# Attention and experts on one core: row-maximum scores for two banks at a time, by the halves of TensorE's rows

## The chip, the cores and the metric

The kernel runs as one program on one core of a Trainium2 chip. The metric is the time of one execution on the device, in microseconds (us); the median of three runs before the change is 1871.49 us.

## The reference

```python
def attn(x, Wq, bq, Wk, bk, Wv, bv, Wo, bo, rel_k, rel_v):      # 16 heads of 8, M = 128
    r = jnp.arange(S)
    idx = jnp.clip(r[None, :] - r[:, None], -M, M) + M
    content = jnp.einsum('bhqd,bhkd->bhqk', q, k)
    relative = jnp.einsum('bhqd,qkd->bhqk', q, rel_k[idx])
    w = jax.nn.softmax((content + relative) / jnp.sqrt(jnp.float32(hd)), axis=-1)
    out = jnp.einsum('bhqk,bhkd->bhqd', w, v) + jnp.einsum('bhqk,qkd->bhqd', w, rel_v[idx])
    ...
x = x + layernorm(attn(layernorm(x), ...))                      # x: 16 x 512 x 128
x = x + layernorm(experts(layernorm(x), ...))                   # top 1 of 16 experts, and a shared one
```

Every query has 16 heads and 512 keys. A key further than 128 positions from its query takes one of two constant relative rows, a nearer one takes the row of its distance.

## The kernel before

There are two phases, each in a block of its own (`nc.Block()`), in which every engine follows its own list and engines wait for each other on semaphores only. The first phase is attention, the second the routed experts.

Attention works on pairs of batches, in eight turns. A turn i has 128 slots. In slot s TensorE computes the scores of one tile of 32 queries against 128 keys, for 16 heads (`scores`, L723 and, where the query tile t = s//32 and the key tile j = s//8%4 differ by at most 1, also L730), ScalarE takes their exponentials (L932), and at every odd slot TensorE multiplies two earlier slots' exponentials with the values (`values`, L749, and L756 for near tiles; its tile lags by one group of eight slots). The scores bank pair is `sc[0]`, `sc[1]`.

The softmax needs the maximum of each row beforehand. In the same slot, for the next turn's batches, `natural` computes the scores of 8 queries by 16 heads (128 rows) against all 512 keys into one bank of `mix`: L704 the content with the keys near the queries, L705 the relative part against the table `Wn`, and L707 and L709 the content with the keys to the left and to the right, which have a constant relative row added. Each has 128 rows of contraction, 128 columns of weights (`Qb`: queries masked by head, `Qn`: queries laid by slots e) and up to 367 moving columns. VectorE reduces the bank to 128 maxima (`row_max`, L1133), after 16 of them writes two halves of them to `ms`, and SyncE stores these (`store_max`, L453).

Two banks `mix[0]` and `mix[1]` serve these jobs in a fixed ring (`shared`, `bank`): "row max" of every slot, and at 16 places of a turn a "prepare" job (transposes and projections of the batch after: L654, L665, L667, L670) or a "finish" job (output projection, second transpose, router logits, counts: L766, L654, L776, L781). Before a job TensorE waits until the engine that empties its bank has done so for the job two places back (`wait_for_bank`): for a row maximum that is VectorE's `mx_done`. "Prepare" jobs are emptied by ScalarE (L885, L889, L893) and, the fourth, by VectorE (L1078).

`natural` of a pair of batches needs `Qb`, filled by ScalarE one head at a time (`by_head`, L923, 16 activations for 32 queries of each slot e), and `Qn`, loaded by SyncE's queue from `qn_d` in 8 DMAs (`load_qn`, L433). SyncE's queue is one in-order list of waits and DMAs, written out by slots in `turn`.

Ahead of the eight turns a prologue computes the maxima of the first two batches (128 times `natural` and `row_max`) over four banks. In the last turn there is no next pair, and no `natural`.

## Time and profile before

| | us |
|---|---|
| three runs | 1867.78, 1871.49, 1873.87 |
| the profiled execution, device time | 1884.98 |
| its span, first to last instruction | 1883.2 |
| TensorE busy | 1660.2 (88%) |
| VectorE busy | 1263.5 (67%) |
| ScalarE busy | 1117.2 (59%) |
| GpSimd busy | 538.3 (29%) |

The profiled execution lies 13.5 us above the median of the runs, and 1.8 us of its time are outside the span. Busy time is the time in which at least one instruction of the engine was running. TensorE's matmuls overlap, so the durations in single rows add up to more than the time they take; the time a step takes on TensorE is read from the start of one row to the start of the next.

### The profile page before, as it was taken

What the parts mean: (1) busy time and instruction counts of PE and PEld (TensorE: products, weight loads), DVE (VectorE), ACT (ScalarE), POOL (GpSimd) and SP (SyncE); (2) the same over time, 40 slices, a digit from 0 to 9 for tenths busy, and PEclk for the clock granted to TensorE, in tenths of its full rate; (3) what the DMA queues carried; (4) which work ended last, traced back from release to release, by engine and by line L of the source; (5) the groups of instructions that cost most, each with busy time, mean ns of one, the idle gap of its engine ahead of it and who ended that gap; (6) DMA issues with size and microseconds to landing.
All of it is one profiled execution on the core that took longest, in us unless ns stands there. A gap on an engine that the chain in (4) does not pass through costs nothing. (4 is left out here: it accounts for less than half of the span.)

```text
span 1883.2 us, 67470 instructions
## 1 busy us (share of the span) xinstructions
PE 1660.2 (88%) x28157; PEld 1380.4 (73%) x28157; DVE 1263.5 (67%) x3502; ACT 1117.2 (59%) x2059; POOL 538.3 (29%) x1114
## 2 busy tenths in 40 slices
PE   2889999999999999999999999999999997486661
PEld 1668878878888888888888887888777754386661
DVE  5996667687787777777878787777733353154454
ACT  2437757675767676667667675767557632174450
POOL 5423031322232223313231323131111145513335
PEclk9999999999999999999999999999999999887876
DMA  2477765755564563446445635453257242143320
GB/s 66 131 176 205 158 172 102 184 121 129 102 145 94 117 134 80 112 96 146 93 129 96 156 47 137 97 139 61 56 111 196 45 122 76 45 114 109 103 79 25
DMA packets 490866, 212.08 MB, mean 113 GB/s; under 512 B 332392, under 2 KB 464165, under 8 KB 490561
## 3 DMA queue, kind: packets, MB, share of 16 engines
q1 hardware_dynamic: 475968, 165.76, 39.9%
q0 software_dynamic: 14592, 42.00, 6.8%
q8 instruction: 222, 3.64, 0.8%
q14 instruction: 84, 0.68, 0.1%
HBM read 105.73 MB, written 102.85 MB: 111 GB/s over the span
## 5 line engine op out<-in xcount | busy, mean ns | idle before, releaser
L932 ACT ACTIVATE w<-sc,escale 128x512 f32<-128x512 f32 x1024 | 690.6, 687 | 435.9 <-PE sc L730 262.1
L1133 DVE TENSOR_REDUCE mx<-mix 128x1 f32<-128x512 f32 x960 | 648.6, 686 | 276.3 <-PE mix L709 203.7
L723 PE MATMUL sc<-QC,KC 104*128 104x128 f16 x4096 | 402.6, 221 | 6.6 <-issue 2.9
L749 PE MATMUL pv<-w,VC 128*9 128x128 f32 x8192 | 386.2, 276 | 6.1 <-issue 6.0
L723 PEld LDWEIGHTS sc<-QC,KC 104*128 104x128 f16 x4096 | 263.9, 99 | 122.4 <-issue 80.4
L704 PE MATMUL mix<-WE 128*128 128x367 f16 (+2 forms) x960 | 313.6, 327 | 24.6 <-DVE mx L1133 15.9
L705 PE MATMUL mix<-Wn,WE 128*128 128x367 f16 (+2 forms) x960 | 285.9, 298 | 0.6 <-issue 0.6
L730 PE MATMUL sc<-QT,Wt 96*128 96x64 f16 x5120 | 261.8, 193 | 7.5 <-issue 7.5
L756 PE MATMUL rel<-w,Rv 128*32 128x128 f32 x5120 | 264.1, 275 | 3.9 <-issue 3.8
L923 ACT ACTIVATE WE<-qp,hmask 128x256 f16<-128x256 f16 x512 | 249.1, 501 | 24.1 <-PE sc L707 14.4
L749 PEld LDWEIGHTS pv<-w,VC 128*9 128x9 f32 x8192 | 176.0, 90 | 69.0 <-issue 51.3
L730 PEld LDWEIGHTS sc<-QT,Wt 96*128 96x128 f16 x5120 | 215.5, 97 | 9.6 <-issue 9.6
L124 POOL TENSOR_TENSOR rtmp<-rstd 128x4 f32<-128x4 f32 x144 | 30.5, 212 | 563.4 <-DVE rstd L118 555.9
L709 PE MATMUL mix<-WE 128*128 128x272 f16 (+3 forms) x720 | 172.3, 239 | 0.0
L704 PEld LDWEIGHTS mix<-WE 128*128 128x128 f16 x960 | 138.4, 144 | 39.4 <-DVE mx L1133 27.3
L707 PE MATMUL mix<-WE 128*128 128x1 f16 (+3 forms) x720 | 161.4, 224 | 1.4 <-issue 1.4
L756 PEld LDWEIGHTS rel<-w,Rv 128*32 128x32 f32 x5120 | 157.0, 111 | 6.6 <-issue 5.7
L705 PEld LDWEIGHTS mix<-Wn,WE 128*128 128x128 f16 x960 | 155.5, 162 | 1.9 <-issue 1.4
L1732 PE MATMUL gu<-sT,we 128*128 128x128 f32 x640 | 101.8, 310 | 49.4 <-ACT sT L1773 42.5
L1732 PEld LDWEIGHTS gu<-sT,we 128*128 128x128 f32 x640 | 92.6, 223 | 54.3 <-ACT sT L1773 46.6
L1701 POOL DMA_INDIRECT out_dram<-og,oidx x80 | 78.8, 985 | 147.6 <-DVE og L1874 125.9
L707 PEld LDWEIGHTS mix<-WE 128*128 128x128 f16 x720 | 103.9, 144 | 9.2 <-issue 1.6
(231 smaller groups left out, 2158.6 us busy)
## 6 DMA issues: line engine op xcount, KB each, us to landing
qm_d<-ks POOLq DMA_DIRECT2D x48, 512.0 KB, 4.6
QT<-qm_d SPq DMA_DIRECT2D x32, 768.0 KB
kt_d<-ks SPq DMA_DIRECT2D x48, 256.0 KB
KC<-kt_d SPq DMA_DIRECT2D x128, 96.0 KB
xs_d<-zrow SPq DMA_DIRECT2D x5, 2056.0 KB, 10.9
vs_d<-vst SPq DMA_DIRECT2D x16, 576.0 KB
VC<-vs_d SPq DMA_DIRECT2D x32, 288.0 KB
orl_d<-rel_s SPq DMA_DIRECT2D x512, 8.0 KB
```

The source lines that it names most:

```text
L704: nc.tensor.matmul(nat[:, lo:hi], lq, kn[b2][:, 0, lo:hi], start=True, stop=False, skip_group_check=True)
L705: mm = nc.tensor.matmul(nat[:, lo:hi], le, Wn[:, x0 + lo:x0 + hi], start=False, stop=True, skip_group_check=True)
L707: mm = nc.tensor.matmul(nat[:, 0:lo], lq, kn[b2][:, 1, 0:lo], start=False, stop=True, skip_group_check=True)
L709: mm = nc.tensor.matmul(nat[:, hi:S], lq, kn[b2][:, 2, hi:S], start=False, stop=True, skip_group_check=True)
L723: mm = nc.tensor.matmul(bank[:, P * g:P * g + P], KC[j][:, b2, g, 0 if near else 1, :], qc[:, g, :, 32 * q8:32 * q8 + 32], start=(g == 0), ...
L730: mm = nc.tensor.matmul(view[:, :, b, :], Wt[:, x0:x0 + P], qt[:, :, NB * q8 + b, :], start=False, stop=(b == NB - 1), skip_group_check=True)
L749: mm = nc.tensor.matmul(pv[b2][32 * g:32 * g + 9, P * hh:P * hh + P], VC[j][:, b2, 0 if near else 1, h, :], wt[:, :, b2, h, :], start=(j = ...
L756: mm = nc.tensor.matmul(rel[k // 4][32 * q32:32 * q32 + 32, P * (k % 4):P * (k % 4) + P], lv, wt[:, q32, :, :, NU * k:NU * k + NU], start= ...
L923: ins = nc.scalar.activation(Qb[half][:, :, h, :].rearrange("p e (t b) -> p e t b", t=2), src, ACT.Copy, scale=hmask[:, h:h + 1])
L932: nc.scalar.activation(w[tile % 2][:, slot % 4, slot // 4 % 2].rearrange("p h q -> p (h q)"), sc[slot % 2][:], ACT.Exp, scale=escale[:, 0: ...
L1133: nc.vector.tensor_reduce(mx[:, k:k + 1], nat[:], AX.X, ALU.max).then_inc(s["mx_done"], 1)
L1732: mm = nc.tensor.matmul(gu[m % 2][:, c, :], we[m % RING][:, P * c:P * c + P], sT[m % 2][:], start=True, stop=True)
```

## The change

`natural` becomes a function of a pair of slots. The 128 rows of contraction are split into two halves of 64: rows 0 to 63 hold heads 0 to 7, rows 64 to 127 heads 8 to 15. The first half writes one bank of `mix`, the second the other. A bank now holds 8 heads by 16 queries, so two banks together hold the same 256 rows as two slots did. Each half has one content matmul over 512 keys and two relative ones ("sides", 8 queries each) over 256 or 384 keys. The keys are kept rotated, with the constant part added to those beyond the diagonal blocks (`kn`, 1024 columns instead of 1536), so one content matmul takes the place of up to three.

The order of a pair of slots becomes: scores, scores, wait for both banks, `natural` for both, values, then the pair's "prepare" and "finish" jobs (before: scores, `natural`, jobs, in each slot, then values). VectorE takes both maxima at the even slot, before its other work of the two slots. ScalarE's `prep` and `finish` steps move behind the odd slot's exponentials. `by_head` does 8 heads instead of 16 with the same number of elements each, written with larger steps. `load_qn` takes 16 DMAs instead of 8, `store_max` 4 instead of 2, the load of `Wn` 16 instead of 8. GpSimd adds two halves of the head mask and clears a smaller `Qn`; one memset on VectorE goes. Both blocks are made with `no_gpsimd_drain=True`.

```diff
 WT_W, WT_0 = 508, 252
-WN_W, WN_0 = 367, 127
+WN_W, WN_0 = 455, 199
+
+
+
+KEYS_AT = (0, P, 3 * P, 4 * P)
+NEAR_BLOCKS = ((0, 2), (0, 3), (1, 4), (2, 4))
+NEAR_OUT = (2 * P, P, 0, 0)
 Z_W, Z_0 = 384, 255
...
-    n16 = NE8 * H * 32
-    Qb = [we16[:, n16 * r:n16 * (r + 1)].rearrange("p (e h q) -> p e h q", e=NE8, h=H) for r in range(2)]
-    Qn = [we16[:, n16 * (2 + r):n16 * (3 + r)].rearrange("p (e h k) -> p e h k", e=NE8, h=H) for r in range(2)]
-    kn = [we16[:, 4 * n16 + 3 * S * r:4 * n16 + 3 * S * (r + 1)].rearrange("p (v k) -> p v k", v=3) for r in range(2)]
-    at = (4 * n16 + 6 * S) // 2
+    n16 = NE8 * H8 * 32
+    Qb = [we16[:, n16 * r:n16 * (r + 1)].rearrange("p (m t s n) -> p m t s n", m=8, t=2, s=2) for r in range(2)]
+    Qn = we16[:, 2 * n16:7 * n16].rearrange("p (n k) -> p n k", k=32)
+    kn = [we16[:, 7 * n16 + 2 * S * r:7 * n16 + 2 * S * (r + 1)] for r in range(2)]
+    at = (7 * n16 + 4 * S) // 2
...
-        shared.append(("row max", slot))
+        if slot % 2 == 0:
+            shared += [("row max", slot), ("row max", slot + 1)]
...
-    block = ctx.enter_context(nc.Block())
+    block = ctx.enter_context(nc.Block(no_gpsimd_drain=True))
...
-            c = OFF0 - WN_0 - 16 * e
-            sp.dma_start(Wn[HD * e:HD * e + HD, 0:WN_W], rpart[0][:, c:c + WN_W]).then_inc(s["sp_set"], 16)
+            c = OFF0 - WN_0 - 8 * e
+            for r in range(2):
+                row = 64 * r + HD * e
+                sp.dma_start(Wn[row:row + HD, 0:WN_W], rpart[0][:, c:c + WN_W]).then_inc(s["sp_set"], 16)
...
-            src = qn_d[bass.ds(c * P, P)].rearrange("(h d) (e k) -> e d h k", d=HD, e=NE8)
-            for e in range(NE8):
-                row = HD * e
-                sp.dma_start(Qn[half][row:row + HD, e, :, :], src[e, :, :, 32 * half:32 * half + 32]).then_inc(qn_ld[half], 16)
+            src = qn_d[bass.ds(c * P, P)].rearrange("(r h d) (e k) -> r e d h k", r=2, d=HD, e=NE8)
+            for r in range(2):
+                for e in range(NE8):
+                    row, col = 64 * r + HD * e, NE8 * H8 * (2 * half + 1) + H8 * e
+                    sp.dma_start(Qn[row:row + HD, col:col + H8, :], src[r, e, :, :, 32 * half:32 * half + 32]).then_inc(qn_ld[half], 16)
...
-            dst = qt_d[bass.ds((2 * n + b2) * H, H)].rearrange("h r (t e b) -> r t e h b", t=NT, e=NE8)
+            at_least(sp, "ms_st", MS_STORES * group)
+            dst = qt_d[bass.ds((2 * n + b2) * H, H)].rearrange("(g h) r (t e m) -> r t g e h m", g=2, t=NT, m=8)
             for part in range(2):
-                sp.dma_start(dst[ROWS_TERM + part, t], ms[:, part, 16 * t:16 * t + 16]).then_inc(s["ms_st"], 16)
+                for r in range(2):
+                    sp.dma_start(dst[ROWS_TERM + part, t, r], ms[:, part, 16 * t + 8 * r:16 * t + 8 * r + 8]).then_inc(s["ms_st"], 16)
...
-        def natural(n, b2, k, nat):
+        def natural(n, b2, pair, nats):
 
             c = 2 * n + b2
-            if k == 0:
+            t, m = pair // 8, pair % 8
+            half = t // 2
+            if pair == 0:
                 pe.wait_ge(s["k_ev"], c + 1)
-            if k % 32 == 0:
-                pe.wait_ge(qn_ld[k // 32], QN_LOADS * (c + 1))
-                pe.wait_ge(s["qb_done"], 2 * c + k // 32 + 1)
-            t, b = k // 16, k % 16
-            lo = max(0, P * t + b - (M - 1))
-            hi = min(S, P * t + b + 16 * (NE8 - 1) + M)
-            lq = Qb[t // 2][:, :, :, 16 * (t % 2) + b].rearrange("p e h -> p (e h)")
-            le = Qn[k // 32][:, :, :, k % 32].rearrange("p e h -> p (e h)")
-            x0 = WN_0 - P * t - b
-            nc.tensor.matmul(nat[:, lo:hi], lq, kn[b2][:, 0, lo:hi], start=True, stop=False, skip_group_check=True)
-            mm = nc.tensor.matmul(nat[:, lo:hi], le, Wn[:, x0 + lo:x0 + hi], start=False, stop=True, skip_group_check=True)
-            if lo > 0:
-                mm = nc.tensor.matmul(nat[:, 0:lo], lq, kn[b2][:, 1, 0:lo], start=False, stop=True, skip_group_check=True)
-            if hi < S:
-                mm = nc.tensor.matmul(nat[:, hi:S], lq, kn[b2][:, 2, hi:S], start=False, stop=True, skip_group_check=True)
-            mm.then_inc(s["nat_ps"], 1)
+            if pair % 16 == 0:
+                pe.wait_ge(qn_ld[half], QN_LOADS * (c + 1))
+                pe.wait_ge(s["qb_done"], 2 * c + half + 1)
+            first, last = NEAR_BLOCKS[t]
+            near = slice(NEAR_OUT[t], NEAR_OUT[t] + P * (last - first))
+            heads = [slice(64 * r, 64 * r + 64) for r in range(2)]
+            lq = Qb[half][:, m, t % 2].rearrange("p s n -> p (s n)")
+            for r in range(2):
+                nc.tensor.matmul(nats[r][:], lq[heads[r]], kn[b2][heads[r], KEYS_AT[t]:KEYS_AT[t] + S], start=True, stop=False, skip_group_check=True)
+            for side in range(2):
+                col = NE8 * H8 * (2 * half + 1 - side)
+                x0 = WN_0 - P * t - 64 * side - m + P * first
+                for r in range(2):
+                    le = Qn[heads[r], col:col + P, 16 * (t % 2) + 8 * side + m]
+                    mm = nc.tensor.matmul(nats[r][:, near], le, Wn[heads[r], x0:x0 + P * (last - first)], start=False, stop=(side == 1), skip_group_check=True)
+                    if side == 1:
+                        mm.then_inc(s["nat_ps"], 1)
...
+                if slot % 2 == 0:
+                    continue
+                both = (slot - 1, slot)
                 if nxt:
-                    wait_for_bank(pe, ("row max", slot), i, prev, nxt, nxt2)
-                    natural(i + 1, slot // 64, slot % 64, bank("row max", slot))
-                for half in range(2):
-                    if (nxt2 if half else nxt) and slot - 64 * half in PREPARE_PE:
-                        job = ("prepare", half, PREPARE_PE[slot - 64 * half])
-                        wait_for_bank(pe, job, i, prev, nxt, nxt2)
-                        prep(i + 1 + half, 1 - half, job[2], bank(*job))
-                if slot % 2 == 1:
-                    for earlier in (slot - 1, slot):
-                        if slot >= 8:
-                            values(i, slot // 8 - 1, earlier % 8)
-                        elif prev:
-                            values(i - 1, 15, earlier)
-                for half in range(2):
-                    if (prev or half == 0) and slot - FINISH[half] in FINISH_PE[half]:
-                        job = ("finish", half, FINISH_PE[half][slot - FINISH[half]])
-                        wait_for_bank(pe, job, i, prev, nxt, nxt2)
-                        finish(i - half, half, job[2], bank(*job))
+                    for one in both:
+                        wait_for_bank(pe, ("row max", one), i, prev, nxt, nxt2)
+                    natural(i + 1, slot // 64, slot % 64 // 2, [bank("row max", one) for one in both])
+                for earlier in both:
+                    if slot >= 8:
+                        values(i, slot // 8 - 1, earlier % 8)
+                    elif prev:
+                        values(i - 1, 15, earlier)
+                for one in both:
+                    for half in range(2):
+                        if (nxt2 if half else nxt) and one - 64 * half in PREPARE_PE:
+                            job = ("prepare", half, PREPARE_PE[one - 64 * half])
+                            wait_for_bank(pe, job, i, prev, nxt, nxt2)
+                            prep(i + 1 + half, 1 - half, job[2], bank(*job))
+                    for half in range(2):
+                        if (prev or half == 0) and one - FINISH[half] in FINISH_PE[half]:
+                            job = ("finish", half, FINISH_PE[half][one - FINISH[half]])
+                            wait_for_bank(pe, job, i, prev, nxt, nxt2)
+                            finish(i - half, half, job[2], bank(*job))
...
-        for k in range(128):
-            at_least(pe, "mx_done", k - 3)
-            natural(0, k // 64, k % 64, (*mix, *sc)[k % 4])
-            if k in PROLOGUE_PE[0]:
-                prologue(0, 1, PROLOGUE_PE[0][k], pv[0])
-            if k in PROLOGUE_PE[1]:
-                prologue(1, 0, PROLOGUE_PE[1][k], pv[1])
+        for pair in range(64):
+            at_least(pe, "mx_done", 2 * pair - 2)
+            natural(0, pair // 32, pair % 32, (mix, sc)[pair % 2])
+            for k in (2 * pair, 2 * pair + 1):
...
-                nc.scalar.copy(kn[b2][:, 0, :], kf[:, 0, :])
-            elif step < 6:
-                v = step - 3
-                nc.scalar.activation(kn[b2][:, v, :], kf[:, 0, :], ACT.Identity, bias=kb[:, v:v + 1])
+                nc.scalar.copy(kn[b2][:, S // 2:3 * S // 2], kf[:, 0, :])
+            elif step == 4:
+                nc.scalar.activation(kn[b2][:, 3 * S // 2:2 * S], kf[:, 0, 0:S // 2], ACT.Identity, bias=kb[:, 1:2])
+            elif step == 5:
+                nc.scalar.activation(kn[b2][:, 0:S // 2], kf[:, 0, S // 2:S], ACT.Identity, bias=kb[:, 2:3])
...
-            src = qp[b2][:, :, 2 * half:2 * half + 2, :]
+            src = qp[b2][:, :, 4 * half:4 * half + 4, :]
+            dst = Qb[half].rearrange("p m t s (e h) -> p h e (t s) m", e=NE8)
             for h in heads:
-                ins = nc.scalar.activation(Qb[half][:, :, h, :].rearrange("p e (t b) -> p e t b", t=2), src, ACT.Copy, scale=hmask[:, h:h + 1])
-            if heads[-1] == H - 1:
+                ins = nc.scalar.activation(dst[:, h], src, ACT.Copy, scale=hmask8[:, h:h + 1])
+            if heads[-1] == H8 - 1:
...
-            nc.vector.tensor_reduce(mx[:, k:k + 1], nat[:], AX.X, ALU.max).then_inc(s["mx_done"], 1)
+            col = 16 * t + 8 * (k % 2) + k % 16 // 2
+            nc.vector.tensor_reduce(mx[:, col:col + 1], nat[:], AX.X, ALU.max).then_inc(s["mx_done"], 1)
...
-                    row_max(i + 1, slot // 64, slot % 64, bank("row max", slot))
+                if nxt and slot % 2 == 0:
+                    for one in (slot, slot + 1):
+                        row_max(i + 1, slot // 64, one % 64, bank("row max", one))
...
-QN_LOADS = 16 * NE8
+QN_LOADS = 16 * 2 * NE8
...
+MS_STORES = 16 * 4
...
-TABLE_LOADS = NE8
+TABLE_LOADS = 2 * NE8
```

## Rows read from the trace of the kernel before

**Rows 1.** The page: TensorE's busy tenths in 40 slices of the span.

```profile
PE   2889999999999999999999999999999997486661
```

**Rows 2.** Busy time by stretches: two middle turns.

```profile
core 0: us, PE busy (x) PEld busy (x) DVE busy (x) ACT busy (x) POOL busy (x), PEclk, DMA share, GB/s
...
844.30:1020.50 176.20, 172.37 (x3342) 145.57 (x3341) 137.61 (x353) 121.95 (x220) 49.30 (x116) 1.00 0.50 113
1020.50:1200.00 179.50, 173.19 (x3342) 145.91 (x3341) 139.99 (x353) 121.84 (x221) 48.52 (x116) 1.00 0.50 111
```

**Rows 3.** TensorE in order of time, a slot pair with far tiles.

```profile
753.43 0.39 PE L723 MATMUL sc<-QC,KC 104*128 104x128 f16 x4
753.65 0.28 PE L704 MATMUL mix<-WE 128*128 128x241 f16 x1
753.77 0.27 PE L705 MATMUL mix<-Wn,WE 128*128 128x241 f16 x1
753.88 0.28 PE L709 MATMUL mix<-WE 128*128 128x271 f16 x1
754.08 0.63 PE L749 MATMUL pv<-w,VC 128*9 128x128 f32 x16
754.64 0.40 PE L723 MATMUL sc<-QC,KC 104*128 104x128 f16 x4
```

**Rows 4.** The same view, a middle query tile (natural over 367 columns).

```profile
708.11 0.35 PE L704 MATMUL mix<-WE 128*128 128x367 f16 x1
...
708.62 0.62 PE L749 MATMUL pv<-w,VC 128*9 128x128 f32 x16
```

**Rows 5.** The same view, near tiles: scores, then natural and values.

```profile
669.43 0.39 PE L723 MATMUL sc<-QC,KC 104*128 104x128 f16 x4
...
669.89 0.30 PE L704 MATMUL mix<-WE 128*128 128x245 f16 x1
...
670.34 0.41 PE L749 MATMUL pv<-w,VC 128*9 128x128 f32 x8
...
671.33 0.34 PE L723 MATMUL sc<-QC,KC 104*128 104x128 f16 x3
```

**Rows 6.** VectorE's maxima and TensorE's wait for them, in order of time.

```profile
60.83 0.67 DVE L1133 TENSOR_REDUCE mx<-mix 128x1 f32<-128x512 f32 x1
...
61.56 0.38 PE L704 MATMUL mix<-WE 128*128 128x367 f16 x1 [0.72 <-DVE mx L1133]
...
753.70 1.29 DVE L1133 TENSOR_REDUCE mx<-mix 128x1 f32<-128x512 f32 x2 [0.60 <-PE mix L709]
```

**Rows 7.** A "prepare" job for the values, and VectorE emptying it.

```profile
694.10 1.16 PE L670 MATMUL mix<-wvT,xnT 128*128 128x128 f32 x8
...
695.30 1.35 DVE L1078 TENSOR_TENSOR vst<-mix,vb 128x512 f32<-128x512 f32 x3 [0.57 <-PE mix L670]
```

**Rows 8.** SyncE's queue ahead of the first `natural`, and what that waited for.

```profile
25.94 5.48 SPq L382 DMA_DIRECT2D Wn<-w  x8
...
32.82 0.92 SPq L388 DMA_DIRECT2D rvp_d<-in_L_attn_rel_v_dram  x1
35.68 0.34 SPq L416 DMA_DIRECT2D qn_d<-qp  x1
36.95 6.46 ACT L923 ACTIVATE WE<-qp,hmask 128x256 f16<-128x256 f16 x16
37.56 7.04 SPq L433 DMA_DIRECT2D WE<-qn_d  x16
43.55 0.39 PE L704 MATMUL mix<-WE 128*128 128x240 f16 x1 [7.07 <-ACT WE L923]
```

**Rows 9.** SyncE's queue: one `store_max` in the middle of a turn.

```profile
734.39 1.20 SPq L453 DMA_DIRECT2D qt_d<-ms  x2
```

**Rows 10.** GpSimd's queue at the end of each block (times min/median/max in ns).

```profile
L106 POOLq DRAIN  x1: 7257/7257/7257, 1640.9 to 1640.9; - x1
...
L108 POOLq DRAIN  x1: 6588/6588/6588, 1876.3 to 1876.3; - x1
```

More of the change, by code:

```diff
@@ L962, in turn @@
                         outputs(i - 1, NT - 1, which)
-                for half in range(2):
-                    if (nxt2 if half else nxt) and slot - 64 * half in prep_at:
-                        step = prep_at[slot - 64 * half]
-                        prep(i + 1 + half, 1 - half, step, bank("prepare", half, min(step, 2)))
                 head = slot % 32 - BY_HEAD[slot // 32]
-                if 0 <= head < H:
+                if 0 <= head < H8:
                     ahead = slot // 32 + 1
@@ L974, in turn @@
                         by_head(i + 2, 0, 0, (head,))
[L975 to L977 removed]
+                if slot % 2 == 0:
+                    continue
+                for one in (slot - 1, slot):
+                    for half in range(2):
+                        if (nxt2 if half else nxt) and one - 64 * half in prep_at:
+                            step = prep_at[one - 64 * half]
+                            prep(i + 1 + half, 1 - half, step, bank("prepare", half, min(step, 2)))
+                    for half in range(2):
+                        if (prev or half == 0) and one - FINISH[half] in finish_at[half]:
+                            finish(i - half, half, finish_at[half][one - FINISH[half]], bank("finish", half, 1))
         for step in range(1, 7):
             prep(0, 0, step, mix[0])
[L981 removed]
+        by_head(0, 0, 0, range(H8))
         for step in range(2):
             prep(0, 1, step, pv[0])
[L984 removed]
+        by_head(0, 0, 1, range(H8))
         for step in range(2, 7):
@@ L987, in _ @@
         for half in range(2):
-            by_head(0, 1, half, range(H))
+            by_head(0, 1, half, range(H8))
         for step in range(7):
             prep(1, 0, step, pv[1])
-        by_head(1, 0, 0, range(H))
+        by_head(1, 0, 0, range(H8))
         turns(act, turn)
@@ L1502, in _ @@
         pool.memset(c15[:], 1.5).then_inc(z, 1)
[L1503 to L1504 removed]
+        for n in range(2):
+            zeros(Qn[:, 160 * n:160 * n + 160])
         pool.wait_ge(z, 1)
```

36 lines of the change are left out of this document (17 added, 19 removed).

## The prediction

> **What bounds the kernel now.** I read the page first. TensorE is busy 9 tenths or more in nearly every slice of the eight turns [rows 1]. By stretches, a middle turn takes 176 to 180 us with TensorE busy for 172 of them, VectorE for 138 to 140 and ScalarE for 122 [rows 2]. So TensorE's order of instructions sets the time, but with a reserve on VectorE of only a fifth. Then I read TensorE in order of time, from the start of a row to the start of the next, since rows overlap. With far tiles a slot is 0.22 us of scores and 0.43 of `natural`, of which about 0.10 is the change to the column tiles of `values`: L709's 271 columns last 0.20, L705's 241 last 0.11. The two slots' values are 0.56 with the way back [rows 3]. In the middle query tiles `natural` takes 0.51 with that change [rows 4], with near tiles 0.45; near scores take 0.46 a slot, near values 0.99 a pair [rows 5]. I take `natural` alone at 0.35 (query tiles 0 and 3) and 0.42 (1 and 2), 64 slots of each a turn: 49.3 us. The last thing to see is the coupling. A maximum takes 0.67 to 0.69, two in a row 1.29 [rows 6]; TensorE starts 0.06 after a maximum has ended (60.83 + 0.67, then 61.56), and VectorE starts some 0.25 after the last column (the maxima at 753.70 reduce the bank whose L709 ended when L723 began at 753.43) [rows 3, 6]. Today that loop hides, since one bank is filled while the other is reduced.
>
> **Matmuls.** A half streams 512 content columns and twice 256 (end tiles) or 384 (middle tiles). At the full clock (1.00 in [rows 2], 2.4 GHz) that is 0.213 + 0.213 = 0.43 and 0.213 + 0.32 = 0.53 us for a pair, if the halves run side by side. The trace has no row halves. The nearest rows are the column tiles: 16 fp32 matmuls of 128 columns, each reported at 0.28 alone, together take 0.56 [rows 3], so four side by side are shown. I take the halves as fully parallel, with 0.03 for the second half's weights. New is also a change of tiling between scores and `natural`, where there was none. Its price lies between 0 and twice the 0.10 of [rows 3]; I take 0.10, the one row there is for such a change. So a pair costs 0.56 or 0.66, a turn 32 x 1.22 = 39.0 us: 10.3 less.
>
> The Trainium skill (TensorEngine Tiling (Array Packing), Key Properties) says that changing the tiling mode drains TensorE while tiles of one mode run independently; the trace agrees for column tiles, with the 0.10. By the first half of that rule the pair is as I cost it; without the drain it would be 0.46 and 0.56.
>
> **The new wait for both banks.** Now both banks are filled at once and emptied one after the other, and TensorE's next `natural` must wait for both. The loop is 0.61 (natural) + 0.20 to 0.25 + 1.29 + 0.06 = 2.16 us at least. TensorE's own pair is 0.46 + 0.61 + 0.10 + 0.56 = 1.73 with far scores and far values, 2.16 or 2.17 with one of them near, 2.6 with both near. Three of a turn's 16 groups of four pairs are far-far: 12 x 0.43 = 5.2 us more a turn. Behind the waiting `natural` on TensorE stand values and the next scores, so ScalarE waits too. VectorE's other work is 137.6 less 64 x 1.29 = 55 us a turn [rows 2, 6], 0.86 a pair, which fits beside the loop on average but comes in lumps: I add 1.5 (bounds 0 and 5).
>
> **The jobs between.** The ring has still two banks. A job behind a pair takes the bank that the next pair needs at once; before, it had a slot of grace. The values' projection ends near 695.2, VectorE empties it by 696.65 [rows 7]: the next `natural` may start 1.5 after the job, its scores fill 0.46, so 1.05 is waited, twice a turn: 2.1. The four steps emptied by ScalarE (some 0.6 to 0.7, as a 512-column activation) wait 0.2 each: 0.8. The two counts stand on VectorE behind the last steps of `finish`: 1.0 each. A job right behind far values must first wait for the pair's own first maximum: 1.6 over a turn. Sum 6.5 (bounds 2 and 9).
>
> A turn thus changes by -10.3 + 5.2 + 1.5 + 6.5 = +2.9 us, seven turns by +20. The eighth has no `natural`.
>
> **Ahead of the turns.** Today the first `natural` starts at 43.55, held by ScalarE's 16 activations, which end at 43.41 [rows 8]. The eight DMAs of `Wn` become 16: 5.5 us more of the queue; 1.9 of it are idle now (32.82 + 0.92 to 35.68), so `qn_d` is stored 3.6 later. The first half's `Qn` loads then end their issue 16 x 0.44 later instead of 8, in all at 48.2 instead of 41.1. They landed by 43.55 today, within 2.5 us. First `natural`: 48.7 to 50.6, so +5 to +7, I take +6. ScalarE's halved `by_head` no longer decides. Behind it the maxima of the prologue are bound by VectorE, as the wait at 61.56 shows [rows 6], and shift whole.
>
> **The ends.** GpSimd's DRAIN takes 7.26 us from 1640.9, with every other engine already waiting; the last one takes 6.59 from 1876.3, to 0.3 before the end of the span [rows 10]. The waits for the stores stand ahead of both. I take both away: -13.8.
>
> **At nothing.** `by_head` goes from 64 to 32 activations a turn of 0.40 (6.46 for 16, [rows 8]), 13 us off ScalarE at most; larger write steps could take that back, not more than double it. ScalarE has 54 us idle in a turn [rows 2]. The shorter `kn` saves 2 x 256 columns there. Each of four `load_qn` has 8 more DMAs (0.44 each), each of eight `store_max` 2 more (0.6 each) [rows 8, 9]: some 14 + 10 us a turn on SyncE's queue. It passes `load_kv` and `load_q` later by up to 5 us; those loads are wanted one or two groups (11 to 23 us) on. If that cover is gone it costs those 5 a turn.
>
> **Sum.** +20 + 6 - 13.8 = +12: the profiled execution's 1885 becomes 1897. It lies 13.5 above the median of the runs, so from 1871.5 I say 1884.
>
> **Rivals.**
> - *Entering the row halves costs nothing.* Each matmul of `natural` starts as the columns ahead of it end (0.12 and 0.11 for 241) [rows 3], so weights load beside them, and nothing need stop. Each pair saves 0.10, 6.4 a turn, of which about 2 drown in VectorE's lumps; a turn gives -1.5, seven -10, the total -18: 1854. This ends faster; the point that decides is an overhead of `natural` of about 0.08 us over its columns. Against it: the 0.10 on the only change in the trace.
> - *The halves overlap only in part.* The column tiles lose nothing [rows 3]; one after the other would lose 0.43 to 0.53. If 0.15 of that is lost, `natural` saves half as much as it did, -5.5 a turn with the loop 0.15 longer in the far pairs: +7 to +10 more a turn, some 1940. The Trainium skill (TensorE: Matmul & The Clock Gate, Measured speedup vs the span model) gives a measured 3.07 for four row tiles side by side, less than four; no trace here shows row tiles.
> - *The change doesn't do what it says*: the halves run one after the other. `natural` is then 0.95 and 1.17 a pair with overheads, 68 a turn instead of 49, and every wait on top, about +24: 2050.
> - *SyncE's queue becomes late*: +5 a turn, 1919. For it: the DMA engines are half busy in each turn [rows 2].
> - *The DRAIN stays* or another takes its place: 1898.
>
> **Numbers.** My forecast 0.40, costless entry 0.29, partial overlap 0.07, one after the other 0.04, queue 0.09, DRAIN 0.07, the rest 0.04. 0.3% is 5.6 us, about what a measurement of this kernel can tell from no change. My forecast's own range is 1872 to 1896, by the bounds of the jobs and lumps; 0.09 of its 0.40 lies within 0.3%. With 0.03 of the costless entry (if jobs cost more) that makes same 0.12; faster is 0.26 of the costless entry and 0.03 of the rest, 0.29; slower 0.59. Range 1850 to 1922 leaves out the two cases of missing overlap and the tail of the queue's.
>
> **What would show it.** A far pair in the turns after: from L723 of one pair to that of the next 2.1 to 2.2 us, with TensorE idle before `natural`, released by VectorE's maximum; a near pair about 2.6, as now less 0.1. The first content matmuls of both halves within 0.05 of each other; from scores' last row to `natural`'s first 0.1 more than now. The turn 177 to 184. The second block beginning 1 us after the last store of the first. The first `natural` at 49 to 50. I am wrong if the far pairs stay at 1.8, if `natural` spans more than 0.8, or if `load_kv` holds the scores at slots 16 or 24.

## The result and the profile after

The kernel after takes 1945.42 us (median of 4 runs, 1941.38 to 1949.81) against 1872.28 us for the kernel before on the same chip: 1.0395 times, 95% interval 1.0366 to 1.0425. It is slower, and by far more than the 1884 us forecast; the range ended at 1922.

The profiled execution after spans 1942.9 us, 59.7 more than the one before. I cut both at the first maximum, at the first exponential of each turn (128 exponentials a turn) and at the last exponential:

| stretch, us | before | after | change | forecast |
|---|---|---|---|---|
| to the first maximum | 44.4 | 51.8 | +7.4 | +6 |
| from there to the first exponential | 91.1 | 97.9 | +6.8 | 0 |
| seven turns | 1243.2 | 1322.6 | +79.4 | +20 |
| the last turn | 131.4 | 126.7 | -4.7 | 0 |
| behind the last exponential | 373.1 | 343.8 | -29.3 | -13.8 |

The windows of two middle turns (columns as in [rows 2]) of the kernel after:

```profile
core 0: us, PE busy (x) PEld busy (x) DVE busy (x) ACT busy (x) POOL busy (x), PEclk, DMA share, GB/s
907.50:1098.10 190.60, 166.06 (x3278) 121.85 (x3276) 137.23 (x353) 129.51 (x188) 48.74 (x116) 0.98 0.47 104
1098.10:1287.90 189.80, 164.26 (x3280) 121.33 (x3278) 137.99 (x354) 129.34 (x189) 48.02 (x116) 0.99 0.49 105
```

TensorE's busy time fell by 6 to 9 us a turn against [rows 2], but it now idles 25 instead of 4 to 6. ScalarE is busier by 7.5 a turn although it has 32 activations fewer. In the page's 40 slices TensorE has eights where [rows 1] has nines:

```profile
PE   2668988888889888888889898988889998858672
```

TensorE and VectorE in order of time, first the start of a pair without a wait, then a whole pair with far tiles (to hold against [rows 3, 6]):

```profile
669.51 0.62 PE L739 MATMUL sc<-QC,KC 104*128 104x128 f16 x8
670.07 0.39 PE L718 MATMUL mix<-WE 64*128 64x512 f16 x2
...
760.90 0.62 PE L739 MATMUL sc<-QC,KC 104*128 104x128 f16 x8
761.87 0.39 PE L718 MATMUL mix<-WE 64*128 64x512 f16 x2 [0.35 <-DVE mx L1158]
762.08 0.50 PE L724 MATMUL mix<-Wn,WE 64*128 64x384 f16 x4
762.52 0.62 PE L765 MATMUL pv<-w,VC 128*9 128x128 f32 x16
763.08 0.40 PE L739 MATMUL sc<-QC,KC 104*128 104x128 f16 x4
...
762.61 1.29 DVE L1158 TENSOR_REDUCE mx<-mix 128x1 f32<-128x512 f32 x2 [0.80 <-PE mix L724]
```

Here every forecast step stands. From one L739 to the next are 2.18 us (forecast 2.1 to 2.2), with an idle 0.35 before `natural`, released by VectorE's maximum. A pair with near scores and near values takes 2.56 (from one pair's first L739, at 1101.54, to the next, at 1104.10; forecast about 2.6). Both content matmuls take 0.21 together (761.87 to 762.08), so the row halves run side by side. From `natural`'s first column to that of the values are 0.65 us; by my terms 0.53 of columns, 0.03 for weights and 0.10 for the change to column tiles are 0.66. The entry shows in the pair without a wait: 0.56 from the start of two slots' scores to `natural` (669.51 to 670.07), where two slots' scores are 0.44 in [rows 3]: 0.12, forecast 0.10.

What was not forecast is in the groups of instructions and in the list of TensorE's waits (engine, line, what it waited for; us in total, times, longest). Three groups of the kernel after, and three of its waits:

```profile
L946 ACT ACTIVATE WE<-qp,hmask 128x256 f16<-128x256 f16 x256 | 353.1, 1447 | 20.2 <-PE sc L724 20.2
L739 PE MATMUL sc<-QC,KC 104*128 104x128 f16 x4096 | 378.6, 222 | 74.3 <-ACT w L955 68.8 <-DVE mx L1158 1.8 <-issue 1.5
L718 PE MATMUL mix<-WE 64*128 64x512 f16 x960 | 193.5, 396 | 113.7 <-DVE mx L1158 58.5 <-DMA WE<-qn_d 13.2 <-issue 12.1
```

```profile
PE sc L739 <- ACT w L955: 68.8, 89, 1.6
PE mix L718 <- DVE mx L1158: 58.5, 108, 4.4
PE mix L718 <- DMA WE<-qn_d: 13.2, 1, 13.2
```

The row to look at is the first: `by_head`'s activation lasts 1447 ns. The same group in the kernel before, with the same 256 elements an activation:

```profile
L923 ACT ACTIVATE WE<-qp,hmask 128x256 f16<-128x256 f16 x512 | 249.1, 501 | 24.1 <-PE sc L707 14.4
```

These are durations. From start to start, where nothing else stands between them, an activation takes 0.40 us before [rows 8] and 1.10 to 1.12 after (eight of them from 37.62, last one included, take 9.17). TensorE now waits 68.8 us in all for exponentials (L955), in 89 places.

Runs for the experiments were made on three other chips, on which the kernel before takes 1768.99, 1768.63 and 1765.43 us, some 103 less than here. In the profiled executions the stretch behind the last exponential differs by 86 (373.1 here, 287.3 there in two kernels with the same second block); why is not known. Each ratio is to the kernel before on the run's own chip.

### The profile page after: what moved, and what is told of

Read it like the earlier page. It is cut to its first block and busy times, and to the rows that moved or that the text cites. A ratio compares the mean times of both kernels' runs of the same rounds, so it can differ in the third digit from the quotient of the medians.

```text
span 1942.9 us, 67022 instructions
## 1 busy us (share of the span) xinstructions
PE 1582.3 (81%) x27645; PEld 1172.5 (60%) x27645; DVE 1262.3 (65%) x3501; ACT 1178.9 (61%) x1803; POOL 535.4 (28%) x1115
## 5 line engine op out<-in xcount | busy, mean ns | idle before, releaser
L955 ACT ACTIVATE w<-sc,escale 128x512 f32<-128x512 f32 x1024 | 710.0, 732 | 411.6 <-PE sc L746 221.1
L1158 DVE TENSOR_REDUCE mx<-mix 128x1 f32<-128x512 f32 x960 | 616.2, 683 | 356.1 <-PE mix L724 347.4
L739 PE MATMUL sc<-QC,KC 104*128 104x128 f16 x4096 | 378.6, 222 | 74.3 <-ACT w L955 68.8
L946 ACT ACTIVATE WE<-qp,hmask 128x256 f16<-128x256 f16 x256 | 353.1, 1447 | 20.2 <-PE sc L724 20.2
L739 PEld LDWEIGHTS sc<-QC,KC 104*128 104x128 f16 x4096 | 246.1, 99 | 192.3 <-ACT w L955 102.5
L718 PE MATMUL mix<-WE 64*128 64x512 f16 x960 | 193.5, 396 | 113.7 <-DVE mx L1158 58.5
L724 PE MATMUL mix<-Wn,WE 64*128 64x256 f16 (+1 forms) x1920 | 219.2, 304 | 0.9 <-issue 0.9
L724 PEld LDWEIGHTS mix<-Wn,WE 64*128 64x128 f16 x1920 | 142.4, 140 | 38.3 <-issue 7.4
L718 PEld LDWEIGHTS mix<-WE 64*128 64x128 f16 x960 | 51.1, 93 | 164.4 <-DVE mx L1158 83.2
L1506 POOL DMA_INDIRECT xs_d<-xs,spot_u x64 | 67.6, 1056 | 115.2 <-DVE spots L1317 75.8
L1797 ACT COPY we<-WE 128x768 f32 x80 | 66.3, 832 | 29.2 <-issue 13.5
```

The source lines that it names most:

```text
L718: nc.tensor.matmul(nats[r][:], lq[heads[r]], kn[b2][heads[r], KEYS_AT[t]:KEYS_AT[t] + S], start=True, stop=False, skip_group_check=True)
L724: mm = nc.tensor.matmul(nats[r][:, near], le, Wn[heads[r], x0:x0 + P * (last - first)], start=False, stop=(side == 1), skip_group_check=True)
L739: mm = nc.tensor.matmul(bank[:, P * g:P * g + P], KC[j][:, b2, g, 0 if near else 1, :], qc[:, g, :, 32 * q8:32 * q8 + 32], start=(g == 0), ...
L946: ins = nc.scalar.activation(dst[:, h], src, ACT.Copy, scale=hmask8[:, h:h + 1])
L955: nc.scalar.activation(w[tile % 2][:, slot % 4, slot // 4 % 2].rearrange("p h q -> p (h q)"), sc[slot % 2][:], ACT.Exp, scale=escale[:, 0: ...
L1158: nc.vector.tensor_reduce(mx[:, col:col + 1], nat[:], AX.X, ALU.max).then_inc(s["mx_done"], 1)
```

## The experiments

My first theory was that the lone 2-byte writes of `by_head` cost what the forecast missed. The rivals were SyncE's longer queue and the order by pairs.

**The kernel after with short runs in `Qb`.** `Qb` is laid so that `by_head` writes runs of 8 elements (16 bytes), in two activations of 128 elements a head instead of one of 256.

```diff
-    Qb = [we16[:, n16 * r:n16 * (r + 1)].rearrange("p (m t s n) -> p m t s n", m=8, t=2, s=2) for r in range(2)]
+    Qb = [we16[:, n16 * r:n16 * (r + 1)].rearrange("p (s n t m) -> p s n t m", s=2, t=2, m=8) for r in range(2)]
...
-            lq = Qb[half][:, m, t % 2].rearrange("p s n -> p (s n)")
+            lq = Qb[half][:, :, :, t % 2, m].rearrange("p s n -> p (s n)")
...
-                ins = nc.scalar.activation(dst[:, h], src, ACT.Copy, scale=hmask8[:, h:h + 1])
+                for side in range(2):
+                    ins = nc.scalar.activation(dst[:, h, side], src[:, side], ACT.Copy, scale=hmask8[:, h:h + 1])
```

> The changed kernel, with Qb laid out so that ScalarE's by_head writes runs of 8 elements (16 bytes) instead of lone elements 512 bytes apart; for that each head takes two activations of 128 elements instead of one of 256, and TensorE reads its weights at a step of 16 elements. Theory A (the lone elements make by_head 1.45 us instead of 0.5, ScalarE is late with the exponentials and TensorE waits in the groups in which by_head lies): the two halves take 0.3 to 0.4 us each, a turn falls from 189 to 176 to 180 us, the kernel from 1945 to 1860 to 1875. Rival B (the wait for both banks and the changes of tiling cost the time): the turn stays at 186 or more, the kernel at 1925 or more. Rival C (SyncE's longer queue holds the loads): as B, and TensorE's waits lie at the loads.

Measured: 1797.39 us, ratio 1.0155 (1.0131 to 1.0179). **The kernel after unchanged**, on another of these chips, to hold it against:

> The changed kernel once more, beside the kernel before on the same chip as the two runs with it, so that shares can be told apart on one chip. All theories: ratio 1.04 as before. Turns 2 to 6 at 189 to 191 us where those of the kernel with runs of 8 elements took 177 to 179; the difference to that kernel, 2.4% of the time, is by_head.

Measured: 1856.53 us, ratio 1.049 (1.0471 to 1.0509). By the two ratios the write form is worth 59 us of the kernel's 88. TensorE's reading of `Qb` doesn't explain the gain: the content matmul's row became longer with the new layout (mean 438 ns, before that 396). The same group and two middle turns, in the kernel with short runs:

```profile
L947 ACT ACTIVATE WE<-qp,hmask 128x128 f16<-128x128 f16 x512 | 172.1, 394 | 28.0 <-PE sc L724 28.0
```

```profile
872.80:1049.80 177.00, 163.23 (x3281) 123.33 (x3279) 135.23 (x353) 111.46 (x220) 48.92 (x116) 1.00 0.50 112
1049.80:1227.70 177.90, 163.28 (x3280) 123.37 (x3278) 136.73 (x353) 111.54 (x221) 48.51 (x116) 1.00 0.51 112
```

The mean of turns 1 to 6 is 177.6 us against 186.4 in the kernel after on these chips, 9 less, and ScalarE is busy 18 less a turn. Where in a turn that time lay is seen in windows of eight slots in which `by_head` runs (slots 1 to 8, 42 to 49, 70 to 77, 110 to 117 of the fourth turn). First the kernel after (its first trace), then the one with short runs:

```profile
718.00:734.50 16.50, 12.95 (x298) 10.13 (x298) 12.47 (x44) 15.01 (x20) 2.40 (x12) 1.00 0.69 124
779.90:793.70 13.80, 12.44 (x270) 9.86 (x268) 11.15 (x27) 13.80 (x17) 2.75 (x12) 1.00 0.26 35
817.40:832.10 14.70, 11.30 (x187) 8.25 (x188) 8.37 (x23) 14.70 (x20) 0.00 (x0) 0.90 0.27 42
880.40:894.00 13.60, 9.87 (x189) 6.88 (x188) 9.08 (x26) 13.60 (x16) 0.20 (x1) 1.00 0.45 47
```

```profile
694.20:707.20 13.00, 11.73 (x280) 9.64 (x283) 10.98 (x41) 10.49 (x27) 2.42 (x12) 1.00 0.68 108
752.20:764.30 12.10, 11.78 (x259) 9.43 (x257) 10.80 (x27) 9.66 (x24) 2.16 (x9) 1.00 0.47 73
788.60:799.80 11.20, 10.30 (x194) 8.17 (x195) 8.38 (x23) 10.40 (x28) 0.00 (x0) 1.00 0.26 47
848.10:857.90 9.80, 8.80 (x180) 6.63 (x178) 7.39 (x16) 9.47 (x24) 0.20 (x1) 1.00 0.61 82
```

In the kernel after ScalarE is busy all of 13.80, 14.70 and 13.60 us: in these slots it is the bound. Together they last 58.6 against 46.1 us, and 58.6 in each of turns 1 to 5 in both traces of the kernel after. That is 12.5 us; outside the lumps the kernel after is some 3 us a turn quicker, which leaves the 9. Eight exponentials at 0.6 and eight activations at 1.10 make 13.6.

**The kernel after with `by_head` spread.** The same 32 long activations, but behind every second slot.

```diff
-                head = slot % 32 - BY_HEAD[slot // 32]
-                if 0 <= head < H8:
+                later = slot % 32 - BY_HEAD[slot // 32]
+                head = later // 2
+                if 0 <= head < H8 and later % 2 == 0:
```

> The kernel after, with one line changed: by_head's eight activations stand behind every second slot (16 slots) instead of behind each of 8 slots. Their number, form and price (1.45 us each) stay, so ScalarE's busy time stays. Theory (what counts is ScalarE's demand inside the window, not its idle time in the turn): today a slot of the window wants 0.73 + 1.45 = 2.18 us of ScalarE where TensorE gives it 1.1 to 1.3; spread over pairs, a pair wants 2 x 0.73 + 1.45 = 2.91 us where TensorE needs 2.2 to 2.6. The loss of a window falls from about 3 us to about 1, a turn from 187-189 to 181-183, and the kernel to 1.025-1.035 of the kernel before where the kernel after measured 1.049; the start ahead of the turns stays as in the kernel after. Rival (the long writes hurt by their total, or by disturbing other engines' access to SBUF while they run, wherever they stand): the turns stay at 186 to 190 and the ratio at 1.045 to 1.05.

Measured: 1796.78 us, ratio 1.0181 (1.0161 to 1.0201), the activation unchanged at 1456 ns, and ScalarE as busy as in the kernel after:

```profile
865.80:1044.30 178.50, 161.37 (x3281) 119.89 (x3279) 137.44 (x354) 130.77 (x189) 48.57 (x116) 1.00 0.50 111
```

Yet the turn is as short as with short runs (mean of turns 1 to 6: 177.1 against 177.6). So neither ScalarE's total nor a disturbance of other engines costs it; only the demand inside the eight slots does. It came out better than I expected, because I had added durations (0.73 + 1.45 a slot). Rows of one engine overlap; from start to start the two take about 0.60 and 1.10, so a pair wants 2.3 us of ScalarE, a little over a far pair's 2.18 and less than a near pair's 2.56. What is left is small: TensorE's waits for exponentials are 17.5 us in all, against 65.9 in the kernel after on these chips.

**The kernel before with scattered writes.**

```diff
-    Qb = [we16[:, n16 * r:n16 * (r + 1)].rearrange("p (e h q) -> p e h q", e=NE8, h=H) for r in range(2)]
+    Qb = [we16[:, n16 * r:n16 * (r + 1)].rearrange("p (q e h) -> p e h q", e=NE8, h=H) for r in range(2)]
```

> The kernel before, with one line changed: Qb is laid with the query outermost, so by_head's 64 activations of a turn write the same 256 elements each, lone 2-byte elements 256 bytes apart, instead of runs of 32. Nothing of the change's order, queue or natural. Theory (the write form alone costs it): the activation goes from 0.50 to 1.4-1.6 us, a slot in the 16-slot windows wants 2.2 us of ScalarE instead of 1.2, where TensorE gives 1.3 to 1.4; each of four windows loses 10 to 14 us, a turn 40 to 50 us, the start ahead of the turns 10 to 20, the kernel is at 1.15 to 1.22 of the kernel before. Rival (the price in the kernel after came from the change's four-dimensional pattern or its place beside the halves, not from lone elements): the activation stays under 0.8 us and the ratio within 1.00 to 1.03. TensorE's weight load of Qb becomes contiguous here, which may take a little off natural.

Measured: 1954.77 us, ratio 1.107 (1.1046 to 1.1095). The write form alone, with none of the change around it, costs 189 us; the activation's mean is 1465 ns. The size is below my range for the reason just given. ScalarE in order of time, inside a window:

```profile
770.26 1.46 ACT L923 ACTIVATE WE<-qp,hmask 128x256 f16<-128x256 f16 x1
771.21 0.94 ACT L932 ACTIVATE w<-sc,escale 128x512 f32<-128x512 f32 x1
772.03 1.43 ACT L923 ACTIVATE WE<-qp,hmask 128x256 f16<-128x256 f16 x1
772.96 0.93 ACT L932 ACTIVATE w<-sc,escale 128x512 f32<-128x512 f32 x1
773.77 1.52 ACT L923 ACTIVATE WE<-qp,hmask 128x256 f16<-128x256 f16 x1
```

From one L923 to the next are 1.75 us (770.26, 772.03, 773.77), less than 1.46 + 0.94. Sixteen of them take 28 us, and the sixteen slots of a window, with ScalarE's other work, 30.3 on average, where the kernel before without DRAINs (below) takes 23.5. So the four windows lose 27 us, and turns 1 to 5 are 24 longer than there.

**Two probes of write forms.** Both leave out the whole computation; an engine writes 256 elements a partition (in one form 128), several instructions of each form in a row.

> A kernel of ScalarE's copies alone (it leaves out the whole computation and stores x as the output): 256 f16 elements from 8 x 4 x 8 in each of ten forms, eight times each: contiguous; steps of 2, 8 and 32 elements; the changed kernel's own form (innermost step 512 bytes); the same places with the innermost step 16 bytes; runs of 32; the own form in f32; contiguous writes with a stepped read; runs of 8. Theory A: the own form takes about 1.45 us and the contiguous 0.5; if the price is one of lone 2-byte elements, every stepped form takes it, also step 2; if it is one of the step's size, it grows from step 2 to 32; if it is one of the number of dimensions, the runs pay it as well.

> A probe by itself; it leaves out the whole computation and copies x to the output. ScalarE writes 256 f16 elements with a scale, eight of each form in a row: contiguous; lone elements every 8 bytes (four of them); runs of 2 elements every 32 bytes apart from each other in 16 runs' places (4 bytes every 32); runs of 4 (8 bytes every 64); lone f32 elements every 32 bytes. Then VectorE copies the same 256 f16 elements contiguous and as lone elements every 16 bytes, then GpSimd the same two. If the price is that of a written word shared between two activations' elements (a write smaller than 4 bytes), then lone f16 at 8 bytes takes 1.1 us a piece like the 16-byte ones, and runs of 2, runs of 4 and lone f32 take 0.4 to 0.5. If it is a price per separate run beyond some step, runs of 2 take about half of 1.1, runs of 4 a quarter above the contiguous, and lone f32 1.1. On VectorE: 0.1 to 0.3 us contiguous; no expectation for the lone form, the two theories give the same.

They took 60.98 and 38.12 us. ScalarE in order of time in the first; "step" is 8 activations each at steps of 2, 8 and 32 elements, "own" the form of the kernel after and the same places with another order of dimensions, the first "runs" runs of 32, "wide" the form of the kernel after in f32, "turned" a stepped read written contiguously, the last "runs" runs of 8 with 128 elements each, as in the kernel with short runs:

```profile
2.02 3.30 ACT L49 ACTIVATE plain<-src,scale 128x256 f16<-128x256 f16 x8
5.22 21.59 ACT L49 ACTIVATE step<-src,scale 128x256 f16<-128x256 f16 x24
26.34 18.42 ACT L49 ACTIVATE own<-src,scale 128x256 f16<-128x256 f16 x16
44.27 3.48 ACT L49 ACTIVATE runs<-src,scale 128x256 f16<-128x256 f16 x8
47.66 4.16 ACT L49 ACTIVATE wide<-src,scale 128x256 f32<-128x256 f16 x8
51.63 4.95 ACT L49 ACTIVATE turned<-src,scale 128x256 f16<-128x256 f16 x8
56.49 2.43 ACT L49 ACTIVATE runs<-src,scale 128x128 f16<-128x128 f16 x8
```

The eight at a step of 2 take 3.4 of the 21.59 us, so the other sixteen take 1.14 each, like "own" (18.42/16 = 1.15). A row's total also holds the overlap of its last activation, so the prices below are taken between the starts of single activations, which these merged rows don't show and which are a little less. The second probe: lone f16 elements every 8 bytes, runs of 2 and of 4 f16, lone f32 every 32 bytes, then VectorE and GpSimd, contiguous and lone every 16 bytes:

```profile
5.24 2.54 ACT L52 ACTIVATE lone<-src,scale 128x256 f16<-128x256 f16 x4
7.53 6.45 ACT L52 ACTIVATE runs<-src,scale 128x256 f16<-128x256 f16 x16
13.89 4.28 ACT L52 ACTIVATE lone<-src,scale 128x256 f32<-128x256 f16 x8
18.20 1.18 DVE L69 COPY v_plain<-src 128x256 f16<-128x256 f16 x8 [18.20 <-ACT lone L52]
19.29 4.69 DVE L71 COPY v_lone<-src 128x256 f16<-128x256 f16 x8
24.04 2.81 POOL L37 COPY g_plain<-src 128x256 f16<-128x256 f16 x8 [23.06 <-DVE v_lone L71]
26.79 9.23 POOL L39 COPY g_lone<-src 128x256 f16<-128x256 f16 x8
```

So 256 elements cost 0.40 us contiguous or in runs of 2 and more, and 0.42 at a step of 2; 0.49 to 0.51 as lone f32; 0.57 as lone f16 every 8 bytes; 1.11 to 1.14 every 16 bytes or more. (A stepped read with a contiguous write, "turned", costs 0.61.) So not every lone 2-byte write pays, and beyond 16 bytes the price no longer grows with the step. Neither theory of the second probe holds whole: it isn't a price per separate run (runs of 2 and lone f32 are nearly free), and lone f16 at 8 bytes doesn't pay in full.

The Trainium skill (SBUF — State Buffer, Specifications (TRN2)) says that SBUF has lines of 16 bytes and that an access pattern needs at least two hits in a line for full bandwidth. The probe agrees where lone f16 at 16 bytes cost 1.13 and runs of 2 at 32 bytes 0.40; it differs for lone f32 every 32 bytes, one hit a line at only 0.51, and for f16 every 8 bytes, two hits at 0.57. Which part of the chip makes the price is not shown.

**The number of DMAs alone.** The kernel before, with `Wn` in 16 DMAs, `load_qn` in 16 and `store_max` in 4 (each DMA cut in two), nothing else.

```diff
-                sp.dma_start(Qn[half][row:row + HD, e, :, :], src[e, :, :, 32 * half:32 * half + 32]).then_inc(qn_ld[half], 16)
+                for r in range(2):
+                    heads = slice(8 * r, 8 * r + 8)
+                    sp.dma_start(Qn[half][row:row + HD, e, heads, :], src[e, :, heads, 32 * half:32 * half + 32]).then_inc(qn_ld[half], 16)
```

> The kernel before with the changed kernel's number of DMAs and nothing else of it: load_qn 16 DMAs of half the heads instead of 8, store_max 4 of half the columns instead of 2, the load of Wn 16 of half the rows instead of 8. Theory Q (SyncE's queue is what costs the start: in the kernel with runs of 8 the first maximum is 7.2 us later and the first two turns take 23 us more than with the DRAIN alone gone): the first maximum at 50 to 52 instead of 44.4, the first turns 10 to 20 us longer together, the later ones within 1 us, ratio 1.010 to 1.018. Rival (the long first turns come from the pairing of the slots): only the 7 us of the start, ratio 1.004.

Measured: 1787.64 us, ratio 1.011 (1.0092 to 1.0129). The first maximum comes 6.1 us later than in the kernel before without DRAINs (below), the first exponential 9.5, and turn 0 is 10.4 longer; turn 1 is 1.2 longer, and the mean of turns 1 to 6 is 174.4 against 174.1. So the queue costs some 20 us, nearly all of it in the first 325 us. Where turn 0 loses them is seen on VectorE (the rows about its longest wait) and in SyncE's queue:

```profile
268.87 0.69 DVE L1138 TENSOR_REDUCE mx<-mix 128x1 f32<-128x512 f32 x1 [1.34 <-PE mix L714]
280.23 1.04 DVE L1161 TENSOR_TENSOR oA<-oA,oB 128x512 f32<-128x512 f32 x1 [10.67 <-DMA xr<-in_L_attn_x_dram]
281.19 0.68 DVE L1138 TENSOR_REDUCE mx<-mix 128x1 f32<-128x512 f32 x1
```

```profile
257.48 7.55 SPq L511 DMA_DIRECT2D orl_d<-rel_s  x16
...
267.39 0.81 SPq L525 DMA_DIRECT2D oA<-opv_d  x1
...
270.95 0.66 SPq L528 DMA_DIRECT2D xr<-in_L_attn_x_dram  x1
```

In the kernel before without DRAINs that load (L523 there) is issued at 245.97, 25 us earlier, 9.5 of which are the later start. VectorE's list is in order: while it waits for the first "finish" job's input it takes no maximum, and TensorE stands before `natural` for 10.2 us. The waits name VectorE there; the cause is SyncE's queue. The same wait for `xr` is in every kernel with the longer queue, but its length depends on what else is in the kernel: 10.7 us here, 12.8 with short runs, 6.8 with the spread `by_head`, and only 2.3 and 2.5 in the two traces of the kernel after, in which `by_head` has held turn 0 up already.

**The order alone.** The kernel before, with the old `natural` twice behind two slots' scores, both maxima at the even slot, the jobs behind.

```diff
-        shared.append(("row max", slot))
+        if slot % 2 == 0:
+            shared += [("row max", slot), ("row max", slot + 1)]
...
+                if slot % 2 == 0:
+                    continue
+                both = (slot - 1, slot)
                 if nxt:
-                    wait_for_bank(pe, ("row max", slot), i, prev, nxt, nxt2)
-                    natural(i + 1, slot // 64, slot % 64, bank("row max", slot))
+                    for one in both:
+                        wait_for_bank(pe, ("row max", one), i, prev, nxt, nxt2)
+                    for one in both:
+                        natural(i + 1, slot // 64, one % 64, bank("row max", one))
```

> The kernel before with the changed kernel's order alone: scores, scores, wait for both banks, two of the old natural, values, then the jobs; VectorE's two maxima at the even slot, ScalarE's steps behind the odd one. No row halves, no change of by_head, of DMAs or of DRAINs. Theory (the pairing costs what my sum says: 6.5 us of waits of the jobs a turn and a loop that the far pairs just reach, since the first bank can be emptied while the second is filled): middle turns 181 to 184 instead of 174 to 176, ratio 1.025 to 1.035. Rival (the pairing is free, and what is left over in the changed kernel is the row halves themselves): turns within 1 us of before, ratio 1.000 to 1.004.

Measured: 1800.13 us, ratio 1.0182 (1.0168 to 1.0195). Turns 1 to 6 take 179.6 on average against 174.1 without the order; the last turn, which has no `natural`, is 7.4 shorter. This came out smaller than expected; why the last turn gains is not settled. TensorE is busy for 173 us of a middle turn here and for 161 to 163 in the kernels with the row halves; so the order by pairs costs some 5.5 us a turn, and the rest of the change gives 2 to 2.5 of them back (177.6 and 177.1).

**The kernel before without DRAINs.**

```diff
-    block = ctx.enter_context(nc.Block())
+    block = ctx.enter_context(nc.Block(no_gpsimd_drain=True))
```

> The kernel before with no_gpsimd_drain=True in both blocks and nothing else. Theory (the two DRAINs of GpSimd lie on the path, 7.26 and 6.59 us): 13.8 us less, 1858, ratio 0.993. If more than the DRAINs goes with the flag (in the changed kernel everything behind the last exponentials took 343.8 instead of 373.1 us, 29 less): 1843, ratio 0.984. If something takes the DRAIN's place: 1872.

Measured: 1752.99 us, ratio 0.9917 (0.9898 to 0.9935), 16 us less. Its stretch behind the last exponential takes 272.7 us, that of the kernels with DRAINs 287.3 (both of the number of DMAs and of the order). So the flag is worth the two DRAINs and not the 29.3 us that this stretch lost on the first chip. It is the fastest kernel of this study.

A summary by stretches, in us, of the profiled executions on the three other chips:

| kernel | first maximum | first exponential | turn 0 | mean of turns 1 to 6 | last turn | behind |
|---|---|---|---|---|---|---|
| before, no DRAINs | 44.4 | 134.5 | 169.8 | 174.1 | 126.8 | 272.7 |
| before, more DMAs | 50.5 | 144.0 | 180.2 | 174.4 | 128.5 | 287.3 |
| before, order by pairs | 44.6 | 135.6 | 174.4 | 179.6 | 119.4 | 287.3 |
| before, scattered `Qb` | 56.2 | 166.1 | 196.8 | 196.2 | 126.1 | 287.3 |
| after | 51.7 | 150.2 | 188.2 | 186.4 | 122.8 | 275.1 |
| after, short runs | 51.6 | 148.9 | 185.8 | 177.6 | 123.0 | 276.6 |
| after, spread `by_head` | 52.0 | 151.7 | 179.8 | 177.1 | 120.0 | 275.8 |

## Why the prediction was wrong

**The step that failed** is the first of "At nothing": `by_head` at 0.40 us, "larger write steps could take that back, not more than double it", and "ScalarE has 54 us idle in a turn". Both parts failed, and no rival of the prediction was about `by_head`. The write steps cost 1.10 in place of 0.40 from start to start, 2.8 times. And idle time in a turn was the wrong cover: the activations stand in four lumps, one a slot, and inside a lump the cover is what TensorE leaves of a slot, 1.2 to 1.6 us (9.8 to 13.0 for eight) less 0.6 for the exponential. At 0.40 they fit, at 0.80, the bound that I gave, they would about have, and at 1.10 they don't. The kernels with short runs and with the spread show each half by itself: either gives back nearly the whole (59 and 55 us of 88, by the ratios).

**The second failure** is the cover of SyncE's queue, "wanted one or two groups on". It held in turns 1 to 6 and not ahead of them and in turn 0, where the queue runs almost without a gap: about 20 us in all when the queue alone is changed, 6 of which I had. The wait fell not on `load_kv`, where I looked, but on the inputs of a "finish" job and, through VectorE's order, on the maxima. "The maxima of the prologue shift whole" was wrong too: from the first maximum to the first exponential the kernel after takes 6.8 more. The queue alone makes 3.4 on the other chips, and what the pairs add beyond that I did not take apart. The windows show only that VectorE, busy for 88.2 of 91.1 us before, is busy for 90.5 of 97.9 after, and that TensorE's mean granted clock in this stretch is 0.95 before, 0.89 with the DMAs alone and 0.79 after, where TensorE waits for a maximum far more often (25 us in all against 9).

**Matmuls** were right, one by one: halves side by side, `natural` with its way back 0.65, and 0.12 for the change of tiling ahead of it, forecast 0.10. A middle turn of the kernel before without DRAINs, in windows:

```profile
828.20:1002.40 174.20, 171.67 (x3343) 145.45 (x3341) 137.24 (x353) 122.11 (x221) 48.60 (x116) 1.00 0.51 114
```

TensorE is busy for 171.7 us there and for 163.2 with short runs: 8.5 less, forecast 10.3. Its idle time grew from 2.5 to 13.8 (14.6 in the second turn shown), some 11.7 more, forecast 13.2 for the loop, the lumps and the jobs. So the net of a middle turn, forecast +2.9, is +3.5 and +3.0 in the two kernels in which `by_head` is not the bound. That it is so near is in part luck: both terms came out 1.5 to 2 us smaller than forecast, and the misses cancel. The far pair at 2.18 us is the loop that I worked out. (With near scores and far values my terms add up to 2.19, not to the 2.16 or 2.17 that I wrote; nothing hangs on it.) The rivals of a costless entry, of halves that overlap in part, and of halves one after the other are refuted by the same rows; the rival of a late SyncE queue was half right, with another place.

**The ends** were right: 14.6 us between the kernels with and without DRAINs, forecast 13.8, and no other wait takes their place. The -29.3 in the table of the first chip is another matter. There the second block took 235.0 us before, 6.6 of it the DRAIN, at a granted clock of 0.78, and 214.0 after at 0.83; on the other chips it takes 159 us in the kernel after and in the kernel before without DRAINs alike. So some 14 us of the -29.3 are not shown to belong to the change; they are about what the profiled execution before lies above its median, 13.5. That the change costs 73 us on the first chip and 88 on the others lies in the turns: seven of them grew by 79.4 us on the first and by 92.4 on the others (1214.3 to 1306.7), where a turn of the kernel before is some 4 us shorter. In the kernel after GpSimd's queue at the end of the first block has, in the view of [rows 10], no DRAIN left:

```profile
L113 POOLq EVENT_SEMAPHORE  x2: 17/17/17, 1728.8 to 1728.9; - x2
L113 POOLq COMPARE_BRANCH  x1: 46/46/46, 1728.6 to 1728.6; - x1
```

**The start**: first `natural` at 50.74, 0.14 beyond the forecast's 48.7 to 50.6 (its own terms, 48.2 and a landing within 2.5, allow 50.7), and released by a load of `Qn`, as forecast. It needs the first half's 16 of the 32 loads in the queue; the last of them was issued from 49.11 to 49.41.

In sum, on the other chips: the writes of `by_head` 59 us, the queue 20, the pairs with the row halves some 3 in each of seven turns, 22, the DRAINs -16; that is 85 of the 88 measured, and the rest is not assigned. The parts are worth this in one order only: the last three build the kernel with short runs up from the kernel before, and `by_head` comes on top. As the wait for `xr` shows (2.3 to 2.5 us in the kernel after, 12.8 without the long writes), a shorter queue in the kernel after, with `by_head` as it is, can be expected to give back less than 20; that was not tried.

## What to carry to other kernels

Cover is to be read in the window where the work stands, not in the turn: how much of each slot is left on the engine that does it, and what waits behind it. When a layout is turned so that one engine reads it well, price the writer's new form by a measurement; in the probe two elements next to each other are enough to avoid the price on ScalarE (the kernel was tried with eight). Price an engine's work from start to start, since durations of neighbouring rows overlap.

## What was not expected of the hardware

From start to start ScalarE writes 256 lone f16 elements a partition in 1.13 us where contiguous ones take 0.40, at a step of 16 bytes, in 1.11 at one of 64 bytes, and in 1.11 to 1.14 in the change's own places in either order of dimensions; 4-byte elements in the change's pattern take 0.49, runs of two f16 0.40. VectorE pays 0.57 instead of 0.14 and GpSimd 1.13 instead of 0.34. The Trainium skill (ScalarE: Activation LUTs, What ACT_TABLE_LOAD costs) gives about 280 ns and 0.833 ns an element for an activation with a pointer operand, 493 ns for 256; the contiguous row agrees with 492 to 501, the lone one, at 1447, does not.
